# An attention kernel: both heads' outputs in one tile for a single projection, and half of the row scalings on ScalarE

## What is computed

```
xn = layernorm(x) * g_in
q  = (xn @ Wq) / 8, 16 heads;  k, v = split(xn @ Wkv)          # one k, v for all heads
s  = q @ [null_k, k]^T + [null_bias, bias], masked, causal
p  = softmax(s);  o = p @ [null_v, v]                          # per head, 64 wide
y  = concat(o over heads) @ Wo
```

## Time and profile before

| | |
|---|---|
| median of 3 runs | 1331.17 us (1330.85 to 1332.63) |
| profiled execution, its own time | 1329.25 us |
| its span, first to last instruction | 1327.5 us |
| TensorE busy in the span | 1002.6 us (76%) |
| VectorE | 802.7 us (60%) |
| GpSimd | 740.6 us (56%) |
| ScalarE | 628.2 us (47%) |

### The profile page before, as it was taken

The page is one execution under the profiler, slowest core; times in us unless marked ns, Lnnn a source line. Parts: engine busy times, 40 slices in busy tenths (PEclk is TensorE's granted clock), DMA queues, the critical chain, the costliest instruction groups (busy, mean ns, idle before and its releaser), DMA issues. The chain is left out here.

```text
span 1327.5 us, 23485 instructions
## 1 busy us (share of the span) xinstructions
PE 1002.6 (76%) x6466; PEld 874.2 (66%) x6467; DVE 802.7 (60%) x2155; ACT 628.2 (47%) x1483; POOL 740.6 (56%) x864
## 2 busy tenths in 40 slices
PE   4859999999999999999998034767725454089986
PEld 3638888888888888878887034667723343078885
DVE  6137767677676767766675574866636756634442
ACT  1126665676666666666665022333312121466553
POOL 1138778888788887878785014505520452624343
PEclk9759999999999999999999555878868676589998
DMA  6154545556555555555550601313338011234443
GB/s 166 53 173 124 167 148 159 168 152 180 147 157 178 153 174 153 156 163 157 149 151 11 217 6 62 102 43 124 119 129 338 32 67 38 96 66 76 65 77 38
DMA packets 111587, 163.70 MB, mean 123 GB/s; under 512 B 16023, under 2 KB 85143, under 8 KB 110456
## 3 DMA queue, kind: packets, MB, share of 16 engines
q1 hardware_dynamic: 100406, 143.21, 36.0%
q0 software_dynamic: 10560, 19.18, 6.2%
q10 hardware_dynamic: 514, 0.04, 0.0%
HBM read 111.68 MB, written 25.53 MB: 103 GB/s over the span
## 5 line engine op out<-in xcount | busy, mean ns | idle before, releaser
L1707 POOL TENSOR_SCALAR probs<-probs,inv_sum 128x1024 f32<-128x1024 f32 (+7 forms) x256 | 439.3, 1729 | 125.5 <-DVE inv_sum L1842 125.3
L1757 ACT ACTIVATE probs<-probs,neg_max 128x1025 f32<-128x1025 f32 (+7 forms) x256 | 200.9, 785 | 115.4 <-POOL probs L1696 107.8
L1810 DVE CUSTOM_DVE_ANT_0 probs<-s_ps,bias_set,neg_null 128x512 f32<-128x512 f32 (+3 forms) x256 | 166.0, 649 | 112.2 <-PE s_ps L1871 110.2
L1739 ACT ACTIVATE pT_hi<-t_ps 128x512 fp32r<-128x512 f32 (+1 forms) x320 | 177.2, 554 | 70.0 <-PE t_ps L1902 69.6
L1832 DVE TENSOR_TENSOR pT_lo<-t_ps,pT_hi 128x512 fp32r<-128x512 f32 (+1 forms) x320 | 201.9, 632 | 11.7 <-ACT pT_hi L1739 11.5
L1922 PE MATMUL o_ps<-pT_hi,values 128*128 128x256 f32 x576 | 174.1, 322 | 23.7 <-DVE pT_lo L1832 22.8
L1902 PE MATMUL t_ps<-ident,probs 128*128 128x128 f32 x1152 | 180.3, 275 | 12.3 <-POOL probs L1707 6.5
L1870 PE MATMUL s_ps<-k_hi,q_hilo 128*128 128x512 f32 (+3 forms) x384 | 161.3, 420 | 8.8 <-DMA q_one<-q_hi 7.5
L1902 PEld LDWEIGHTS t_ps<-ident,probs 128*128 128x128 f32 x1152 | 140.7, 141 | 39.4 <-issue 7.9
L1923 PE MATMUL o_ps<-pT_lo,values 128*128 128x256 f32 x576 | 150.6, 281 | 0.0
L1871 PE MATMUL s_ps<-k_lo,q_one 128*128 128x512 f32 (+3 forms) x384 | 136.0, 354 | 0.0
(11 more groups left out here) (301 smaller groups left out, 2075.6 us busy)
## 6 DMA issues: line engine op xcount, KB each, us to landing
bias_set<-bias_dram SPq DMA_DIRECT2D x16, 1024.0 KB, 5.1
bias_set<-bias_dram SPq DMA_DIRECT2D x16, 896.0 KB, 5.0
bias_set<-bias_dram SPq DMA_DIRECT2D x16, 768.0 KB, 4.8
bias_set<-bias_dram SPq DMA_DIRECT2D x16, 640.0 KB, 4.4
q_hilo<-q_hi SPq DMA_DIRECT2D x128, 64.0 KB, 2.0
q_hilo<-q_lo SPq DMA_DIRECT2D x128, 64.0 KB, 2.0
q_one<-q_hi SPq DMA_DIRECT2D x128, 64.0 KB, 2.0
bias_set<-bias_dram SPq DMA_DIRECT2D x16, 512.0 KB, 5.2
```

The lines of the kernel that those rows point to most:

```text
L1707: last = pool.tensor_scalar(keys, keys, inv_sum[:, x.set, unit, h:h + 1], None, ALU.mult)
L1739: act.activation(pT_hi[n % 3][:, 0:count, :], t_ps[TURNS["slot", n] % 3][:, 0:2 * P * count], ACT.Copy).then_inc(hi_out, 1)
L1757: act.activation(p, p, ACT.Exp, scale=-1.0, bias=neg_max[:, x.set, row.unit, h:h + 1], accum_out=row_sum[:, x.set, row.unit, h:h + 1]).the ...
L1810: dve.tensor_tensor_reduce(probs_row(x, row, h)[:, 1 + P * first:1 + P * (first + count)], s_ps[e % 2][:, 0:P * count], bias_row(x, row, h ...
```

## The change

- `outputs`: ScalarE copies only rows 64 to 127 of `o_ps`, the low halves, to rows 0 to 63 of a new tile `o_low`. VectorE then adds `o_ps` rows 0 to 63 and `o_low`, one instruction per head, the first head to rows 0 to 63 of `oT`, the second to rows 64 to 127.
- `project`: one matmul with `oT` of 128 columns and `wo`, which now holds `Wo` once, by pair of heads. TensorE does it one slot later, behind the first scores chunk of slot n where the tile ended in slot n - 2.
- Short tiles' rows: `normalise_short` on ScalarE, in slot 1 of the step ahead, behind the long tile's first Exp. GpSimd keeps the long rows, and the null weights of both.
- Setup: one load of `Wo`, `nv` loaded into both halves of the partitions, `null_wo` with 8 matmuls.

```diff
-        oT = [sbuf(st, f"oT{i}", [P, 2 * P]) for i in range(2)]
+        oT = [sbuf(st, f"oT{i}", [P, P]) for i in range(2)]
+        o_low = [sbuf(st, f"o_low{i}", [DH, 2 * P]) for i in range(2)]
...
-                    for h in range(2):
+                    for h in range(2) if unit == 0 else ():
                         keys = probs_row(x, row, h)[:, 1:]
                         last = pool.tensor_scalar(keys, keys, inv_sum[:, x.set, unit, h:h + 1], None, ALU.mult)
...
                 def outputs(x, row):
-                    wait(act, projected, units_done(x.g, row.unit) - 2)
+                    wait(act, oT_ready, units_done(x.g, row.unit) - 2)
                     act.wait_ge(pv_done, SLOTS_A_STEP * x.g + (len(x.rows[0].slots) if row.unit == 0 else SLOTS_A_STEP))
-                    act.activation(oT[row.unit][:], o_ps[row.unit], ACT.Copy).then_inc(oT_ready, 1)
+                    act.activation(o_low[row.unit][:], o_ps[row.unit][DH:P, :], ACT.Copy).then_inc(o_low_ready, 1)
...
+                def normalise_short(g):
+                    x = ALL[g]
+                    row = x.rows[1]
+                    act.wait_ge(inv_ready, units_done(g, 1))
+                    apart(act, marks_act)
+                    for h in range(2):
+                        keys = probs_row(x, row, h)[:, 1:]
+                        act.activation(keys, keys, ACT.Copy, scale=inv_sum[:, x.set, 1, h:h + 1]).then_inc(short_normed, 1)
...
                     for x, row, h in EXPS_AT[n]:
                         exps(x, row, h)
+                    if n % SLOTS_A_STEP == 1 and n // SLOTS_A_STEP + 1 < STEPS:
+                        normalise_short(n // SLOTS_A_STEP + 1)
...
+                def outputs(x, row):
+                    wait(dve, projected, units_done(x.g, row.unit) - 2)
+                    dve.wait_ge(o_low_ready, units_done(x.g, row.unit))
+                    for h in range(2):
+                        cols = slice(P * h, P * h + P)
+                        last = dve.tensor_tensor(oT[row.unit][DH * h:DH * h + DH, :], o_ps[row.unit][0:DH, cols], o_low[row.unit][:, cols], ALU.add)
+                    last.then_inc(oT_ready, 1)
...
-                for n in range(NS):
-                    for item in SCORES_AT[n]:
+                for n in range(NS + 1):
+                    for item in SCORES_AT.get(n, ()):
                         fill(item)
                     low(n + 1)
-                    for x, row, h in EXPS_AT[n]:
+                    ended = ends_at(n - 1)
+                    if ended:
+                        outputs(*ended)
+                    for x, row, h in EXPS_AT[n] if n < NS else ():
                         if h:
                             invert(x, row)
...
-                    for h in range(2):
-                        last = pe.matmul(y_ps[:, row.unit, :], oT[row.unit][:, P * h:P * h + P], wo[:, 2 * x.pair + h, :],
-                                         start=(first and h == 0), stop=False, skip_group_check=True)
-                    last.then_inc(projected, 1)
+                    pe.matmul(y_ps[:, row.unit, :], oT[row.unit][:], wo[:, x.pair, :],
+                              start=first, stop=False, skip_group_check=True).then_inc(projected, 1)
...
                         for item in SCORES_AT[n][:1]:
                             fill(item)
+                    ended = ends_at(n - 2)
+                    if ended:
+                        project(*ended)
+                    if n < NS:
                         turn(n + 2)
                         for item in SCORES_AT[n][1:]:
                             fill(item)
                         weigh(n)
-                    ended = ends_at(n - 1)
-                    if ended:
-                        project(*ended)
...
-                    wo_h = Wo.rearrange("(h d) n -> d h n", d=DH)
-                    for half in range(2):
-                        sp.dma_start(wo[DH * half:DH * half + DH, :, :], wo_h).then_inc(wo_in, 16)
+                    sp.dma_start(wo[:], Wo.rearrange("(h p) n -> p h n", p=P)).then_inc(wo_in, 16)
...
-                    act.dma_start(nv[:], cond[1:2, :].rearrange("o d -> d o")).then_inc(small_in, 16)
+                    for h in range(2):
+                        act.dma_start(nv[DH * h:DH * h + DH], cond[1:2, :].rearrange("o d -> d o")).then_inc(small_in, 16)
...
-                        for h in range(H * (g - 1) // 3, H * g // 3) if g else ():
-                            last = pe.matmul(nwps[0:H, 0:D], nv_at[:, h, :], wo[0:DH, h, :], start=(h == 0), stop=(h == H - 1))
+                        for h in range(PAIRS * (g - 1) // 3, PAIRS * g // 3) if g else ():
+                            last = pe.matmul(nwps[0:H, 0:D], nv_at[:, h, :], wo[:, h, :], start=(h == 0), stop=(h == PAIRS - 1))
```

More of the change, by code:

```diff
@@ L1608, in attention_stage @@
         q_hi_ready, q_in = sem("q_hi_ready"), [sem(f"q_in{i}") for i in range(SETS)]
-        inv_ready, normed, null_w_ready = sem("inv_ready"), sem("normed"), sem("null_w_ready")
+        inv_ready, normed, short_normed, null_w_ready = sem("inv_ready"), sem("normed"), sem("short_normed"), sem("null_w_ready")
+        marks_act = sem("marks_act")
         turn_ready, hi_out, t_read, pv_done = sem("turn_ready"), sem("hi_out"), sem("t_read"), sem("pv_done")
-        oT_ready, projected, null_turned, y_ready, y_out = (
-            sem("oT_ready"), sem("projected"), sem("null_turned"), sem("y_ready"), sem("y_out"))
+        oT_ready, o_low_ready, projected, null_turned, y_ready, y_out = (
+            sem("oT_ready"), sem("o_low_ready"), sem("projected"), sem("null_turned"), sem("y_ready"), sem("y_out"))
         marks_sp, marks_pool, marks_dve = sem("marks_sp"), sem("marks_pool"), sem("marks_dve")
@@ L1772, in _ @@
                             exps(x, row, h)
+                normalise_short(0)
                 high(0)
@@ L1897, in turn @@
                     if k == 0:
-                        pe.wait_ge(normed, 2 * units_done(x.g, row.unit))
+                        pe.wait_ge(short_normed if row.unit else normed, 2 * (x.g + 1))
                     wait(pe, t_read, at - 2)
@@ L1987, in program @@
         values = sbuf(attn, "values", [P, NT, P], F32R)
-        wo = sbuf(attn, "wo", [P, H, D])
+        wo = sbuf(attn, "wo", [P, PAIRS, D])
         neg_null = sbuf(attn, "neg_null", [P, NT, H])
@@ L2002, in program @@
             nab_b = sbuf(st, "nab_b", [P, H])
-            nv = sbuf(st, "nv", [DH, 1])
-            nv_at = sbuf(st, "nv_at", [DH, H, H])
+            nv = sbuf(st, "nv", [P, 1])
+            nv_at = sbuf(st, "nv_at", [P, PAIRS, H])
             nk_prod = sbuf(st, "nk_prod", [P, DC, H, DH])
@@ L2041, in _ @@
                     act.dma_start(nk_b[:], cond[0:1, :].broadcast_to([P, DH])).then_inc(small_in, 16)
-                    act.dma_start(nv[:], cond[1:2, :].rearrange("o d -> d o")).then_inc(small_in, 16)
+                    for h in range(2):
+                        act.dma_start(nv[DH * h:DH * h + DH], cond[1:2, :].rearrange("o d -> d o")).then_inc(small_in, 16)
                     act.dma_start(nab_b[:], nab.rearrange("(o h) -> o h", o=1).broadcast_to([P, H])).then_inc(small_in, 16)
                     act.dma_start(mask8[DH:DH + 1, :], mask).then_inc(small_in, 16)
-                    act.wait_ge(small_in, 16 * 5)
+                    act.wait_ge(small_in, 16 * 6)
                     for g in range(4):
@@ L2094, in _ @@
                         last.then_inc(xh_ready, 1)
-                    dve.wait_ge(small_in, 16 * 5)
+                    dve.wait_ge(small_in, 16 * 6)
                     dve.tensor_scalar(k_lo[DH:DH + 1, 0:T], mask8[DH:DH + 1, :], MASKED, -MASKED, ALU.mult, ALU.add)
@@ L2099, in _ @@
                     dve.wait_ge(step0, 10)
-                    dve.tensor_copy(nv_at[:].rearrange("d a b -> d (a b)")[:, 0:H * H:H + 1],
-                                    nv[:].broadcast_to([DH, H])).then_inc(nv_ready, 1)
+                    for h in range(2):
+                        mine = slice(DH * h, DH * h + DH)
+                        last = dve.tensor_copy(nv_at[mine].rearrange("d a b -> d (a b)")[:, h:PAIRS * H:H + 2],
+                                               nv[mine].broadcast_to([DH, PAIRS]))
+                    last.then_inc(nv_ready, 1)
                     dve.wait_ge(wq_all_in, 16)
@@ L2145, in _ @@
                             pe.wait_ge(nv_ready, 1)
-                            pe.wait_ge(wo_in, 32)
+                            pe.wait_ge(wo_in, 16)
                         if g == 2:
                             pe.wait_ge(w_null_ready, 1)
-                        for h in range(H * (g - 1) // 3, H * g // 3) if g else ():
-                            last = pe.matmul(nwps[0:H, 0:D], nv_at[:, h, :], wo[0:DH, h, :], start=(h == 0), stop=(h == H - 1))
+                        for h in range(PAIRS * (g - 1) // 3, PAIRS * g // 3) if g else ():
```

(1 more changed line is left out.)

## The result

The changed kernel takes 1398.41 us (median of 4 runs, 1397.72 to 1402.04), the kernel before 1331.01 (4 runs); the ratio is 1.0499, with a 95% interval of 1.0462 to 1.0536. Forecast were 1347 and a range of 1321 to 1366. The profiled execution took 1402.04 us, its span is 1400.3.

The account below looks back on a forecast made before the run. A ring of ScalarE, VectorE and GpSimd bounds 8-block steps, TensorE the others, with the ring deciding after the change. Steps +27.8, round ends -7.6, setup -3.7, first short rows -1.0, end +0.4: +15.9, about 1347 us; range 1321 to 1366.

Parts of the forecast that it names:

- TensorE's 0.68: Projection in the attention steps: half the weight loads saves TensorE 0.68 us a step, 44 us over 64 steps.
- the 0.57: VectorE's pair of additions per tile: 0.57 us without overlap, added to steps of 6 and 5 blocks only.
- the first ring: ScalarE, VectorE and GpSimd waiting for each other through Exps, reciprocal, long scalings and `put_null`: 9.82 us in 8-block steps.
- the forecast's four steps: Attention steps after the change: 10.42, 9.81, 10.18 and 10.17 us for 8, 7, 6 and 5 blocks.
- The round ends: Extra time at 7 round ends: 13.6 us before, 6.0 after, a gain of 7.6 us.
- the 1.1 taken off for two steps: First two 6-block steps run beside slots of 7-block tiles, without the 0.57: sum 27.8 us instead of 28.9.
- the rival of cheap scalings and additions: ScalarE's scalings at their lower bound and VectorE's additions overlapping: 1321 to 1337 us; chance 0.15.
- the -3.7 of the setup: TensorE's setup ahead of attention: 16 of 32 `nwps` matmul records fall away, 3.7 us of 7.4 saved.
- VectorE's additions delaying also the steps with 8 and 7 blocks: Each pair's 0.57 us coming through once in those 30 steps: +17 us, 1364 us; chance 0.12.
- The rival of the falling clock: TensorE's granted clock falls as its gaps grow to over 1 us a step: 40 us or more; chance 0.04.
- The rival that TensorE would set the step: Attention steps fall with TensorE's shorter stream: 1300 to 1318 us, 1286 at the best; chance 0.13.
- The signs: 8-block Exps 10.4 us apart, waiting for `put_null`; GpSimd's reciprocal wait up over 2 us; TensorE's `pT_lo` wait up about 1.

Follow-up runs that it names:

- e2: Changed kernel with the projection moved behind the slot's weighing on TensorE, at the end of the slot; ratio 1.0069 to the kernel before, 1357.3 us.
- e9: Changed kernel with VectorE's additions ahead of `pT_lo`, projection left in place; ratio 1.0125 to the kernel before, 1348.5 us.
- e12: Changed kernel with GpSimd's null copies issued ahead of its long scalings; ratio 1.0521 to the kernel before, 1401.0 us.
- e1: Changed kernel with the short rows scaled by GpSimd again; ratio 1.0489 to the kernel before, 1416.3 us.
- e3: Kernel before with only the short rows' scalings moved to ScalarE (`normalise_short`); ratio 1.0078 to the kernel before, 1359.0 us.
- e10: Changed kernel with the projection behind the weighing and GpSimd's null copies ahead of its long scalings; ratio 0.9774 to the kernel before, 1302.4 us.
- e5: Changed kernel with short rows back on GpSimd and the projection behind the slot's weighing; ratio 0.9831 to the kernel before, 1323.0 us.
- e11: Changed kernel with short rows on GpSimd, projection behind the weighing and null copies ahead of the long scalings; ratio 0.9744 to the kernel before, 1297.0 us.
- e4: Kernel before with only the projection moved one slot later, ahead of the transposes; ratio 0.9991 to the kernel before, 1348.8 us.
- e8: Kernel of e5 with VectorE's additions behind the reciprocal and GpSimd's null copies ahead of its long scalings; ratio 0.9760 to the kernel before, 1314.3 us.
- e7: Kernel before with only GpSimd's null copies issued ahead of its long scalings; ratio 0.9992 to the kernel before, 1343.9 us.

## Why the prediction was wrong, step by step

**The step that failed.** The prediction says: "Both sides have spare time once the ring sets the step (TensorE's 0.68 and its present waits), so I add nothing beyond the 0.57." The sentences ahead of it name the right queues: scores and `pT_lo` behind or ahead of the waiting VectorE, the transposes behind the waiting TensorE. They were weighed as spare time of two engines, not followed around. An engine's spare time does not help when what it waits for is held up by what stands behind its own wait. The ring read above takes 11.06 us and not 10.42; e2 and e9 take it away at either end, and e12 and e1 show that nothing of the first ring is in the time. So the term that was put at nothing was worth 0.65, 0.59, 0.49 and 1.18 us in a step of 8, 7, 6 and 5 blocks.

**Its price.** Between the first Exps of steps 2 and 63 lie 675.6 us (770.62 - 95.03). The plain steps are 14 x 11.07 + 16 x 10.40 + 16 x 10.67 + 15 x 11.35 = 662.4; the forecast's four steps give 618.3. So 44.1 of the error are in the plain steps. The round ends hold 13.2 where 6.0 were forecast, and the 1.1 taken off for two steps did not come: 8.3. About 4 of these are TensorE's clock, see below. Then the start came 7.4 us earlier (102.44 to 95.03) and not 4.7: -2.7. From the last first Exp to the end it is 629.7 us for 622.1, +7.6 and not +0.4: +7.2, of which 4.7 lie ahead of the last result (25.6 for 21.0 us). In e2, with the second ring open, that piece is 20.4 us, so it belongs to the ring too. Sum 44.1 + 8.3 - 2.7 + 7.2 = 56.9, which is the span's 1400.3 less the forecast 1343.4.

**What was right, and shown.** The ring of the earlier trace rows and its growth by the scalings: e3 measured 10.40, 9.79, 9.60 and 9.92 where the same sums gave 10.4, 9.8, 9.6 and 9.9. With the second ring open, the forecast's own steps (10.42, 9.81, 10.18, 10.17) come out as 10.40, 9.79, 10.21 and 10.08 in e2. Its round ends as well: 622.4 us for 61 steps, 616.8 of them plain, leaves 5.6.

**The prices of instructions.** Two scalings of 128 columns put the next start 0.59 later (150.97 to 151.56), forecast 0.60; two of 512 columns 1.23 (646.38 to the next copy at 647.61, by the timeline), forecast 1.20. So the rival of cheap scalings and additions is out. A pair of additions takes 0.57 and the next VectorE instruction starts 0.60 or 0.61 after it (156.16 to 156.77), as taken, with no overlap. The Trainium skill, "VectorE: DVE Perf Modes", section "Two Vector instructions with no wait between them", holds an instruction whose output starts in another quadrant than the one before; the trace agrees: the pair's 0.57 is twice the 0.278 of one, and the next instruction, which writes from row 0 on again, starts only after the pair has ended, while behind a `pT_lo` of 0.68 us the next one starts after 0.60.

**The start.** `nwps` takes 4.0 us for 7.4, the -3.7 of the setup nearly. The rest of the earlier start was forecast as 1.0, for GpSimd's first short rows, and that is not where it comes from: e1 gives these rows back to GpSimd and its first Exp of step 2 comes just as early (95.28), while e3, which takes only them away, has it at 108.03. The start is made in the setup, and TensorE's granted clock is in it, which is told by the third number from the end of such a row as in the earlier trace rows. Here is the stretch in which TensorE makes the keys, first of the kernel before, then of the changed one:

```profile
28.00:56.00 28.00, 28.00 (x156) 19.26 (x155) 3.34 (x5) 5.66 (x10) 0.00 (x0) 0.87 0.00 1
```

```profile
28.00:50.00 22.00, 22.00 (x144) 16.89 (x144) 3.34 (x5) 5.71 (x11) 0.00 (x0) 0.98 0.00 1
```

In both TensorE is busy without a gap. At 0.87 the kernel before loses 28 x 0.13 = 3.6 us there, the changed one at 0.98 loses 22 x 0.02 = 0.4. So by estimate about 3 us of the earlier start are the clock. In e3 the granted clock is 0.50, the lower level, from 40 to 60 us, and the start is the latest of all. One execution of each kernel was profiled; what decides the clock in the setup stays open.

**The rivals.** VectorE's additions delaying also the steps with 8 and 7 blocks was given 0.12; its 0.57 on top of the forecast make 10.99 and 10.38 us for those steps, and measured are 11.07 and 10.40. That was the nearest. It has the right work, the additions, but adds it to the first ring, which is not in the time. That the sums come so close is luck. What spoke against it in the prediction, that ScalarE waits over 2 us for GpSimd, was the mistake: e12 removes that wait whole and nothing is won. It missed the steps with 6 and 5 blocks (+0.49 and +1.18), where a long tile ends a slot earlier; e2 and e9 both give that back.

The rival of the falling clock was given 0.04 for 40 us or more, and a little of it came. The granted clock is 1.00 in the stretch of the earlier trace rows in both kernels, but at two of the seven round ends of the changed kernel it falls to the lower level for some microseconds (0.72 over 184 to 190 us, 0.50 over 534 to 540):

```profile
534.00:540.00 6.00, 6.00 (x27) 5.35 (x27) 0.76 (x4) 2.13 (x6) 0.00 (x0) 0.50 0.08 28
```

Ahead of both falls TensorE had gaps: it was busy for 0.85 us of 182 to 184 and for 1.38 us of 532 to 534. These two steps take 14.47 and 14.55 us. The first is 12.82 in e1, where the clock stays at 1.00; for the second there is the other round-end step with 6 blocks, 12.23. So the clock costs some 4 us here, an estimate from these steps; in the kernel before it is 1.00 from 100 to 720 us.

The rival that TensorE would set the step and the kernel get faster needs, for the whole change, both rings open: e10 is at 0.977, which is 1301 us against a before of 1331, inside that rival's 1300 to 1318. Without the scalings on ScalarE the second ring alone is enough for that: e5 is at 0.983, 1308 us, and with both open e11 is at 0.974, 1297 us. The prediction looked only at one ring in its way. The Trainium skill's "Perfetto Trace Analysis", section "Identifying the Most-Contended Engine", says to optimise first the engine of highest occupancy, and to judge TensorE by its weight loads and the useful work done; by busy matmuls and by weight loads alike that was TensorE before (75.7 and 67.5 of 78 us). Here that did not pay by itself: as the change stood, TensorE's halved projection came with 5.0% more time, and with the projection moved to the end of the slot and the short rows back on GpSimd (e5) it came with 1.7% less.

**The signs.** Those that the prediction gave did not tell the two rings apart. ScalarE still waited for `put_null`, GpSimd's wait for the reciprocal grew by about 3 us a step (89.8 to 216.0 us in 500), the reciprocal came 1.41 behind the second Exp. One did: TensorE's wait for `pT_lo` before `o_ps` was to grow by about a microsecond a step, and fell from 17.2 to 13.6 us in 500; in e2, where the first ring decides, it is 55.2.

**Open.** Behind the last result it takes 604.1 us for 601.1, in stages that the change does not touch. In the traces of e9 to e12 this part takes 603 to 605 us, in those of e1 to e4 618 to 622, in those of e5 to e8 613 to 619; that is where the times of the three groups part, while the steps agree. Why it differs from chip to chip is not known. e3, e4 and e7, made from the kernel before, are not shorter there than their neighbours, so no effect of the change on it shows. Why the steps with 5 blocks lose most was not taken apart either.

## What to carry to other kernels

When a change adds a wait in the middle of an in-order queue, list what stands behind it on the waiting engine and what stands ahead of the producer on its own, and look for one thing that is on both lists; if there is one, a ring has closed, and its length is found by adding start-to-start distances around it, not by the spare time of the engines. Here the wait at the end of a slot, behind everything that others need, left the forecast's steps as they were, and the same wait ahead of it cost 57 us (ratio 1.0499 for 1.0069). A long visible wait (82.5 us for the null copies) may be a follower: take it away alone before believing that it sets the time.

## What the runs showed beyond this

Opening one ring is worth nothing while another is as long: early null copies gave nothing to the kernel before (9.82 to 9.72 us in a quarter of the steps), nothing to the changed kernel, and 0.49 us in each 8-block step in the kernel of e5 (9.82 to 9.33, e11). What an edit brings here depends on what else is in the way.
